# Two routed tiles per turn, with the last 48 FFN rows of both on the two row halves of TensorE

## What is computed

```
scores = softmax(xt @ Wg.T)                          # 16 experts in 4 groups
masked = scores of the best 2 groups, else -inf
topi   = top_k(masked, 4);  weights = scores[topi]   # 4 experts for each token
h = silu(einsum('td,eid->eti', xt, W1)) * einsum('td,eid->eti', xt, W3)   # i: INTER = 176
expert_out = einsum('eti,edi->etd', h, W2)
y = einsum('etd,te->td', expert_out, combine)
z = silu(xt @ Ws1.T) * (xt @ Ws3.T) @ Ws2.T          # shared experts
x = x + y + z
```

## Time and profile before

| what | value |
|---|---|
| median of 3 runs | 396.31 us (396.02 to 399.64) |
| profiled execution, time | 396.77 us |
| profiled execution, span from the first to the last instruction | 395.0 us |
| PE busy | 383.6 us (97%), 2130 instructions |
| DVE, ACT, POOL busy | 245.1 (62%), 160.9 (41%), 181.2 us (46%) |
| mean DMA rate | 210 GB/s |

### The profile page before, as it was taken

The page is one execution under the profiler, slowest core; times in us unless marked ns, Lnnn a source line. Parts: engine busy times, 40 slices in busy tenths (PEclk is TensorE's granted clock), DMA queues, the critical chain, the costliest instruction groups (busy, mean ns, idle before and its releaser), DMA issues.

```text
span 395.0 us, 9044 instructions
## 1 busy us (share of the span) xinstructions
PE 383.6 (97%) x2130; PEld 277.1 (70%) x2131; DVE 245.1 (62%) x684; ACT 160.9 (41%) x487; POOL 181.2 (46%) x225
## 2 busy tenths in 40 slices
PE   6999999999999999999999999999999999999996
PEld 5787788878887546555666765446767777777775
DVE  5775677988986465788645434444346464646466
ACT  3447656555463462101123433333333333334441
POOL 3254333238788474565563333333333343335333
DMA  7974563468869995256377963234374736372737
GB/s 231 351 285 155 184 251 134 146 206 297 317 236 334 420 419 235 97 202 222 106 223 222 322 225 107 87 100 136 122 250 131 243 110 236 116 243 89 268 99 258
DMA packets 37971, 83.09 MB, mean 210 GB/s; under 512 B 5962, under 2 KB 25902, under 8 KB 36016
## 3 DMA queue, kind: packets, MB, share of 16 engines
q1 hardware_dynamic: 31408, 64.83, 49.0%
q0 software_dynamic: 6528, 17.84, 11.6%
HBM read 60.21 MB, written 23.48 MB: 212 GB/s over the span
## 4 chain that ended last, share of the span: by engine, by line
PE 70%; POOL 7%; DVE 7%; DMA 5%; issue 5%; ACT 3%; SPq 1%; DVEq 0%; POOLq 0%; ACTq 0%
PE heads L1441 17%; PE bank L1515 13%; PE heads L1483 9%; PE heads L1327 6%; PE bank L1496 5%; PE bank L1462 4%; PE heads L1451 4%; POOL rows_scratch L682 3%; PE heads L1329 3%; PE heads L1433 3%; DVE kv L756 2%; PE bank L1507 2%; PE bank L1341 2%; DMA toep<-rows_scratch 2%; DVE prod L798 1%
## 5 line engine op out<-in xcount | busy, mean ns | idle before, releaser
L738 POOL DMA_INDIRECT y_scratch<-toep,dest_i x72 | 72.6, 1009 | 111.2 <-DVE dest_i L1184 92.1
L1441 PE MATMUL heads<-experts,toep 128*128 x256 | 86.6, 461 | 0.8 <-DVE toep L1142 0.7
L1327 PE MATMUL heads<-toep,kv 128*128 128x256 f32 x256 | 77.8, 386 | 1.9 <-DVE kv L756 1.3
L682 POOL DMA_INDIRECT rows_scratch<-rows,slot_i x64 | 63.4, 990 | 35.3 <-issue 18.9
L1515 PE MATMUL bank<-experts,toep 88*128 x256 | 66.3, 381 | 0.9 <-DVE toep L1149 0.9
L571 ACT ACTIVATE toep<-heads 128x176 f32<-128x176 f32 x72 | 22.8, 317 | 78.5 <-PE heads L1441 67.6
L1441 PEld LDWEIGHTS heads<-experts,toep 128*128 128x128 f32 x256 | 43.6, 190 | 15.2 <-issue 1.6
L1329 PEld LDWEIGHTS heads<-toep,kv 128*128 128x128 f32 x256 | 48.7, 190 | 6.5
L798 DVE TENSOR_TENSOR prod<-heads,ctx_rep 128x1024 f32<-128x1024 f32 x32 | 39.1, 1222 | 18.9 <-PE bank L1341 17.6
L1149 DVE COPY toep<-heads 88x256 f32<-88x256 f32 x72 | 30.2, 419 | 30.9 <-PE heads L1451 30.7
L1329 PE MATMUL heads<-toep,kv 128*128 128x128 f32 x256 | 49.2, 274 | 0.0
(11 more groups left out here) (246 smaller groups left out, 506.3 us busy)
## 6 DMA issues: line engine op xcount, KB each, us to landing
ctx_rep<-ctxr_in SPq DMA_DIRECT2D x15, 1024.0 KB, 5.0
experts<-experts_in SPq DMA_DIRECT2D x16, 608.0 KB
toep<-rows_scratch SPq DMA_DIRECT2D x56, 144.0 KB
prod<-y_scratch SPq DMA_DIRECT2D x5, 1024.0 KB, 5.8
rows_scratch<-pad_row SPq DMA_DIRECT2D x17, 144.0 KB, 1.8
ctx_tr<-ctxt_in SPq DMA_DIRECT2D x16, 128.0 KB, 5.5
toep<-toep_in SPq DMA_DIRECT2D x4, 512.0 KB, 7.7
ctx_n<-ctx_in SPq DMA_DIRECT2D x16, 128.0 KB, 2.0
```

The lines of the kernel that those rows point to most:

```text
L682: pool.indirect_dma_start(rows_d, bass.IndirectOffsetOnAxis(ap=slot_i[:, u, k:k + 1].bitcast(U32), axis=0), rows[:, u, :], None).then_inc( ...
L738: pool.indirect_dma_start(y_d, bass.IndirectOffsetOnAxis(ap=dest_i[b][:, 0:1].bitcast(U32), axis=0), y_sb[b], None, bounds_check=TOPK * TO ...
L1327: nc.tensor.matmul(y_ps[par][:, i, :], kv[:, q, 0, h * P:(h + 1) * P], toep[:, k, :], start=True, stop=False)
L1441: last = nc.tensor.matmul(up_ps[p], x_tr[p][:, blk, :], up_w(e, blk), start=blk == 0, stop=blk == LB - 1)
```

## The change

W2 has 176 rows for an expert. Before, they stood as two blocks of 88 rows; now as one of 128 (`down_w`) and one of 48 (REM), and the 48 stand twice in SBUF, at partitions 0 to 47 and 64 to 111. Two tiles make a pair. Their hidden tiles are transposed in three transposes instead of four: the first 128 columns of each, and both 48-column rests side by side. In `down`, the rests of both tiles are multiplied by two matmuls of 48 rows, one on PE's rows 0 to 63 and the other on rows 64 to 127, into two PSUM banks; then follow the two of 128 rows. Since the address of the second tile's expert needs a register of its own kind, DVE copies its 48 rows of W2 (`rest_of_w2`) into a fixed place, `w2_rest`.

All engines go by pairs. PE: turn_x(t+2), turn_x(t+3), down(t-2 and t-1), turn_h(t and t+1), up(t+2), up(t+3). `hid`, `hid_tr`, the transposed hidden PSUM tile and `w2_rest` are now single. SP loads the second experts' weights after the gathers of tiles 9, 11, 13, 15 (two), 17, 19, 21 instead of 5, 7, 8, 9, 10, 11, 13, 14, and reads a pair of units back in two halves of 512 KB that stand between gathers of whole pairs. The diff, cut to these parts:

```diff
-            others_at = {5: (0,), 7: (1,), 8: (2,), 9: (3,), 10: (4,), 11: (5,), 13: (6,), 14: (7,)}
+            others_at = {9: (0,), 11: (1,), 13: (2,), 15: (3, 4), 17: (5,), 19: (6,), 21: (7,)}
...
-                store(m - 5, m * 2 - 10, 2)
-                read_back(m - 4, m * 2 - 8, 2, back, back_in, sends)
-                gathers(m, DEPTH, 2 * DEPTH)
+                gathers(m, DEPTH, DEPTH + 2)
+                sp.wait_ge(finished, m - 4)
+                read_half(m - 4, m * 2 - 8, 0, sends)
+                gathers(m, DEPTH + 2, 2 * DEPTH)
+                read_half(m - 4, m * 2 - 8, 1, sends)
+                send_out(m * 2 - 10, 2)
...
+            def routed_pair(t, b, before):      # ACT
+                silu(t, 0)
+                silu(t + 1, 1)
+                if not (isinstance(t, int) and t == LIVE - 2):
+                    src_tr(t + 2, 0)
+                    src_tr(t + 3, 1)
+                if not (isinstance(t, int) and t == 0):
+                    for i in range(2):
+                        store_y(t - 2 + i, i, (b - 2) % DEPTH + i, before if b >= 2 else before - 1)
...
+            def rest_of_w2(t, b):               # DVE
+                if not (isinstance(t, int) and t < 2):
+                    dve.wait_ge(rest_done, pair_of(t))
...
+                e = dve.snap(taken_of[b + 1], min_val=0, max_val=E - 1)
+                nc.vector.tensor_copy(w2_rest[HALF:HALF + REM, :].unsqueeze(1),
+                                      experts[HALF:HALF + REM, bass.ds(e, 1), at:at + L]).then_inc(rest_ready, 1)
+            def copy_h(m):
+                dve.wait_ge(ht_done, m + 1)
...
+                nc.vector.tensor_copy(hid_tr, ht_ps).then_inc(htr_ready, 1)
...
+            def routed_pair(t, b, before):      # DVE
+                hidden(t, 0, b)
+                hidden(t + 1, 1, b + 1)
...
+                        take(t + 2 + i, (b + 2) % DEPTH + i, before + 1 if b == DEPTH - 2 else before)
+                rest_of_w2(t, b)
+                copy_h(pair_of(t))
                 place(t, b, before)
+                place(t + 1, b + 1, before)
...
+                for p in range(2):              # PE, turn_h
+                    nc.tensor.transpose(ht_ps[:, p, :], hid_main[p], ident[:])
+                nc.tensor.transpose(ht_ps[:, 2, :], hid_rest, ident[:]).then_inc(ht_done, 1)
...
+                nc.tensor.matmul(dn_ps[0], hid_tr[rest[0], 2, :], rest_w(e[0]), start=True, stop=False)
+                nc.tensor.matmul(dn_ps[1], hid_tr[rest[1], 2, :], w2_rest[rest[1], :], start=True, stop=False
+                                 ).then_inc(rest_done, 1)
+                for i in range(2):
+                    nc.tensor.matmul(dn_ps[i], hid_tr[:, i, :], down_w(e[i]), start=False, stop=True).then_inc(dn_done, 1)
```

More of the change, by code:

```diff
@@ L157, in build @@
         act1 = [carve(INTER) for _ in range(2)]
-        hid = [carve(INTER) for _ in range(2)]
-        hid_tr = [carve(2 * P)[0:HI, :].rearrange("p (b n) -> p b n", b=2) for _ in range(2)]
+        hid = carve(2 * P + HALF + REM)
+        hid_main, hid_rest = (hid[:, 0:P], hid[:, HALF + P + REM:]), hid[:, P:2 * P]
+        hid_tr = carve(3 * P).rearrange("p (c n) -> p c n", c=3)
+        w2_rest = carve(L)
         y_sb = [carve(L) for _ in range(DEPTH)]
@@ L259, in part, with routed @@
             eng.sem_inc(wait_taken, 1)
[L261 to L266, removed]
+        def routed(step, until, eng):
+            for t in range(0, until, 2):
                 step(t, t % DEPTH, t // DEPTH)
@@ L269, in routed, with pair_of @@
             with eng.Fori(until // DEPTH, static // DEPTH) as it:
-                for b in range(DEPTH):
+                for b in range(0, DEPTH, 2):
                     step(it * DEPTH + b, b, it)
-            for t in range(static, LIVE):
+            for t in range(static, LIVE, 2):
                 step(t, t % DEPTH, t // DEPTH)
+        def pair_of(t):
+            return t // 2
         def is_late(t):
@@ L410, in read_back, with read_half @@
                 sp.dma_start(into.rearrange("p k u l -> p u (k l)"), y_v[:, bass.ds(u0, units), :]).then_inc(signal, 16)
+            def read_half(i, u0, half, sends):
+                read_back(i, u0 + half, 1, back[:, :, half:half + 1, :], back_in, sends)
             def send_out(u0, units):
@@ L441, in _ @@
                         late_gather(late_at[t])
-            for b in range(DEPTH):
-                gathers(4, b, b + 1)
+            gathers(4, 0, DEPTH)
             sp.wait_ge(sends_ready, 1)
-            read_back(0, 0, 2, back, back_in)
-            for b in range(DEPTH):
-                gathers(4, DEPTH + b, DEPTH + b + 1)
+            sends = [sends_of(0, b) for b in range(DEPTH)]
+            gathers(4, DEPTH, DEPTH + 2)
+            read_half(0, 0, 0, sends)
+            for b in range(2):
+                late_gather(DEPTH + b)
+            gathers(4, DEPTH + 2, 2 * DEPTH)
+            read_half(0, 0, 1, sends)
+            for b in range(2, DEPTH):
                 late_gather(DEPTH + b)
@@ L463, in _ @@
             store(3, 6, 2)
-            read_back(4, 8, 2, back, back_in, sends)
+            for half in range(2):
+                read_half(4, 8, half, sends)
             read_back(5, 10, 2, back_ten, ten_in)
@@ L606, in _ @@
             src_tr(0, 0)
[L608 to L616, removed]
+            src_tr(1, 1)
+            def routed_pair(t, b, before):
[7 more added lines that the diff above has]
+                        store_y(t - 2 + i, i, (b - 2) % DEPTH + i, before if b >= 2 else before - 1)
+            routed(routed_pair, 2 * DEPTH, act)
             for t in range(LIVE - 2, LIVE):
```

172 lines of the change are left out of this document (97 added, 75 removed).

## The result

| | median | runs | ratio to before, 95% interval |
|---|---|---|---|
| before | 397.1 us | 11 (396.02 to 399.64) | |
| after | 394.55 us | 11 (392.81 to 397.25) | 0.9933 (0.9907 to 0.996) |
| after, measured again beside another 29 runs of before (396.07) | 394.89 us | 12 (392.38 to 397.79) | 0.9963 (0.9936 to 0.999) |

The account below looks back on a forecast made before the run. The prediction took PE's streaming to bound most of the routed stage. Its terms -3.2 (ordinary pairs), -2.2 (mixed pairs), -2.3 (stalls), +1.7 (end) summed to -6.0, from a median of 396.31 to 390.3 us; range 383 to 397.

Parts of the forecast that it names:

- Ordinary pairs: Pairs of ordinary tiles on PE: 4.88 us instead of 4.98, .10 saved for each of 32 pairs, -3.2 us.
- Rivals 2: Row halves in `down` need no drain: 14 us less, 376; chance .10.
- 3 (halves in turn): Row halves in `down` run one after the other: two passes more, 15.5 us, 405.8, slower; chance .10.
- Mixed pairs: Mixed tiles: PE's pair falls from 6.14 to 5.16 us, but SP's DMAs lag; -2.2 us, between -.6 and -3.9.
- I take half of 3.3 as lost: Mixed pairs: SP falls behind by 3.3 us, half of it counted as lost, giving -2.2 us.
- Stalls: PE's late steps at tiles 5 and 14 and the first read-back (.61, 1.09, .60) all vanish: -2.3 us.
- I take all of it back: The stalls at tiles 5, 14 and the first read-back are wholly regained: -2.3 us, -1 at the least.
- Rival 5: Gathers between half read-backs come later and PE waits: 5 rounds of up to 1 us, 395; chance .06.
- The end: Behind the last `up`: tile 67's send starts 1.9 us later than before, +1.7 us, 0 if as early.
- it becomes 8.7 + 1.7: DVE's wait for the last read-back ends 8.7 us after the last `up` instead of 6.8, then needs 1.7.
- Rival 4 (DVE): DVE becomes the bound through `place` waiting for sends: .5 lost in 14 pairs, 397, no change; chance .16.

Follow-up runs that it names:

- d1_whole: Changed kernel with the two rest matmuls of ordinary pairs on the whole array instead of row halves: 393.04 us, ratio to before 0.9915.
- t2_others: Changed kernel with second experts' weights loaded after the gathers of tiles 5, 7, 8, 9, 10, 11, 13, 14, as before the change: 395.83 us.
- best1: Changed kernel with SP's last read-back register loads early, PE's expert load early, second experts' weights ahead of the mixed gathers: 388.57 us, ratio to before 0.9798.
- again: Second profile of the changed kernel, nothing edited: 394.35 us for the profiled execution, median 394.89 us.
- t1_loads: Changed kernel with SP's 24 register loads for the last six read-backs ahead of the wait for round 3's sums: 392.30 us, ratio 0.9921.
- t3_expert: Changed kernel with PE's register load of a pair's first expert moved to the start of the turn: 392.15 us, ratio 0.991.
- t4_store: Changed kernel with the store of a finished pair of units ahead of the first half read-back instead of behind the second: 393.16 us, ratio 0.9915.

## Why the prediction was wrong, step by step

- **Ordinary pairs: right, and 1 us better.** Predicted 4.88, measured 4.83. That the halves run side by side (.01 apart), that each change of shape costs .20 (taken: .22; bounds .145 and .22) and that `down` therefore gains next to nothing, so that the transpose is the gain, is all in the trace and in d1_whole. The Trainium skill (TensorEngine Tiling (Array Packing), Key Properties) says that a change of tiling mode drains TensorE; the trace agrees that a change has a price, .40 us for the two of a pair. Rivals 2 (no drain) and 3 (halves in turn) fall.
- **Mixed pairs: half right.** PE's part was predicted at 5.16 and is 5.13 to 5.19 when SP keeps up (t2_others, best1). The failed step is "I take half of 3.3 as lost": of the 3.9 that PE gained, 2.8 went (28.3 against 25.5 us for tiles 16 to 26), since SP went at 6.33 a pair and there was almost no lead to live on. I had the row for that price and took it half.
- **Stalls: the old ones went, new ones came.** "I take all of it back": those at tiles 6 and 14 and at the first read-back did vanish (4.83, 4.87 and 4.83 there in `again`; in the first profile 5.20 at the read-back). The step missing from the sum is a register load in front of `up`, with only `turn_h` and `down` queued ahead of it on PE, and how long it takes when transfers crowd: 2.4 us in all. Rival 5 gave 395 for waits of PE in each read-back round. The place and nearly the time came true, but its cause did not: no gather was late, and the time is a coincidence.
- **The end: the failed step that weighs most.** That tile 67's send would start about .5 before the end of the last `up` was right (.4). The failed step is "it becomes 8.7 + 1.7": it kept everything behind the send at what it was before. DVE's wait for unit 15 ends 12.5 us after the last `up` instead of 8.7: 2.1 more for tile 67's landing (4.4 instead of 2.3), 1.5 more from that landing to unit 15's (8.4 instead of 6.9). I moved PE's and POOL's work earlier and left SP where it was. SP's 16 register loads for the last read-backs take 9.5 us (in the first profile of after 368.7 to 378.2) and set when unit 12's read-back goes; before, it went 2.6 us ahead of tile 67's send, now behind it. t1_loads takes the 2.1 away, and the term becomes +2.8 instead of +5.0. Why unit 15's read-back takes longer stays open.
- **The order of the last two `up`: missing from the sum.** The end term is counted from the end of the last `up`, and that end comes 1.3 us earlier by the new order alone. With it the same terms would have given -7.3. So the forecast stood nearer to the measured time by luck.
- **Rival 4 (DVE)**: `place` did wait more for the sends (13 times, 15.8 us in all, 2.2 at the longest in `again`; before), but the steps of t3_expert, 4.83 with these waits in place (15 times, 14.0), show that they were hidden.

With the terms as measured, -.2 - 4.2 - .6 - 1.1 - 1.3 + 5.0 = -2.4. The errors that made it slower are 1.8 for the new waits, 1.1 for the mixed tiles and 3.3 for the end; the better pairs (1.0) and the order (1.3) hid part of them. The first two and 2.1 of the third are of the same kind: work of SP, or a register load, that stood still while the work that I had costed moved.

## What to carry to other kernels

When a change makes the bounding engine faster, go through each in-order queue that didn't change, SP first, and ask at what time its next transfers are issued and what they now meet; a run of register loads in front of a DMA is work for the queue (16 of them took 9.5 us here, .6 each), best put where the queue waits anyway. A register load that the busy engine issues needs cover by the work queued ahead of it, for a duration of the worst case and not of the median. And price both ways of a cleverer shape: here two passes saved were two changes of shape paid, and the plain transpose that the new layout spared was .11 of the .15 that a pair gained.

## What the runs showed of the hardware

- A load of one number from SBUF into a PE register takes .30 us at the median and up to 1.2 or 1.3 while a half read-back, a store, gathers and sends are under way together. The Trainium skill (DMA: Bandwidth & Descriptors, Latency and other measured facts) gives about 600 ns as the floor of a `tensor_load`. The trace disagrees, and the measurement decides: most loads here take half of that.
- Tile 67's indirect send landed 2.3 us after its start in before and 2.5 in t1_loads, and 4.4 and 4.8 in the two profiles of the changed kernel, where 512 KB of read-back were issued within 1 us behind it.
- In the first profile of after, PE stood idle for 3.46 us before the last unit's sum, and in the sum the granted clock fell to half (1.2 GHz, columns here as on the page: stretch, its length, busy time of PE, PEld, DVE, ACT and POOL, granted clock, DMA share, GB/s):

```profile
385.00:388.50 3.50, 0.08 (x1) 0.00 (x0) 2.95 (x7) 0.38 (x1) 0.98 (x1) 1.00 0.99 335
388.50:389.40 0.90, 0.86 (x4) 0.78 (x5) 0.00 (x0) 0.00 (x0) 0.00 (x0) 0.98 1.02 348
389.40:392.50 3.10, 3.03 (x8) 1.86 (x6) 1.61 (x4) 0.04 (x1) 0.00 (x0) 0.50 0.49 171
```

  In `again` PE was idle for 2.88 us at the same place, and the clock stayed at 1.00:

```profile
386.00:388.60 2.60, 2.43 (x10) 1.82 (x10) 0.05 (x1) 0.04 (x1) 0.00 (x0) 1.00 0.98 342
```

  The eight passes took 3.20 us in the one and about 1.8 in the other. The profile of t4_store, where PE was idle for 3.42 us there, shows 0.50 too. So a late transfer at the end can cost twice: the wait, and then the slower sum.
